# First attention of a five-stage kernel: the last 65 keys' output products packed into two matmuls, the denominators into one

## The chip, the cores and the metric

One core of a Trainium2 chip runs the whole kernel; the other cores are idle. The metric is device time in microseconds for one execution: the median of the runs. TensorE appears as PE in the profile (its weight loads as PEld), VectorE as DVE, ScalarE as ACT, GpSimd as POOL, SyncE, which issues most DMAs, as SP.

## The reference

The kernel computes a chain of six residual stages on x (8 batches x 64 rows x 512). Only the first, a grouped cross-attention over a context of 1601 keys per batch, is touched:

```
q = (layernorm(x) @ Wq + bq)  -> 8 groups of 4 heads, head size 128
k, v = split(ctx @ Wkv + bkv) -> 8 key/value heads
attn = softmax(q k^T / sqrt(128)) over the 1601 keys
x = x + (attn @ v) @ Wo + bo
```

The reference is in float32. A state-space stage, a ternary linear layer, an attention against the raw context, a self-attention and an octonion feed-forward layer follow; none of them is changed.

## The kernel before, in words

**Precision.** A float32 operand is split into a high part (rounded to the type `float32r`, which PE multiplies in one pass) and a low part (source minus high). `product` (L57) issues three matmuls: high*high, high*low, low*high (as L59, L60, L61 in the profile).

**Units.** The attention works in 64 units: 8 batches (`b`) times 8 key heads (`j`); a unit is one key head with its 4 query heads' 64 rows, 256 columns (`NQ`). The 1601 keys are 12 chunks of 128 and a last one of 65 (`rows`, L277). Chunks are grouped by two into `NG` = 7 groups and these into four `PIECES`; the last piece is the 65-key chunk alone.

**Work of a unit.** PE makes the keys from the context in four tiles (`key_tile`, 402, 402, 402 and 396 columns), for each pair of units the values (`value_tile`), the scores, and in `attend` the outputs: 13 chunks with three matmuls each, L59 to L61, then the denominators (`denominators`, L584 and L585: ones times the high and the low part of the partial sums). The softmax is done on ACT (copies, exponentials, high parts `pt_hi`), DVE (maxima, subtraction, sums, low parts of keys and values) and POOL (low parts `pt_lo` at L479, `sum_lo` at L492). The values of the 65 last keys were computed before and lie in DRAM; for each pair of units SP loads them with one DMA (L393) and POOL splits them (`split_on_pool`, L1017 and L1019).

**Order.** Each engine's order is written out by hand in a function `group(b, j, last)`, one call for each unit; engines are tied by semaphores. `attend(b, j - 1)` runs in `group(b, j)`: right after the scores when j is odd, after the four key tiles of the next unit when j is even. POOL's order in a group is: weights and queries of unit j + 2 (`key_weights`), for even j the values of the last keys (`rest_values`, which waits for the end of PE's attention), `low`, `sum_low`, for j = 6 the split of the next batch's context (`split_ctx`, L472 and L474, four tiles with two raw buffers: the load of tile 2 waits for the split of tile 0), for even j the value weights (L443, L445). PE's first product with a new context is key tile 0 in the group j = 7, after `attend(b, 6)`; each tile waits for its own split (`ctx_lo_set`). There are seven such changes of batch.

Of the kernel before, what the change touches and what calls it, by code (L numbers as in the profile page):

```python
# [70 lines left out]
class Context:  # L71


    def __init__(self, nc, scope, ctx_t):
# [7 lines left out]
        self.pad_set, self.hi_set, self.lo_set = (scope.sem(n) for n in ("pad_set", "hi_set", "lo_set"))  # L82
# [177 lines left out]
def cross_attention(nc, context, early, rest, output, s_ps, st, wk, wv, ident, q_dram, o_dram):  # L260
# [47 lines left out]
    with Scope(nc, "xa") as sc:  # L308
# [66 lines left out]
        def _(sp):  # L375
# [63 lines left out]
        def _(pool):  # L439
# [24 lines left out]
            def split_ctx(b, n):  # L464

                for t, (c, w) in enumerate(TILES):
# [4 lines left out]
                    raw, hi, lo = context.parts(t)  # L471
                    nc.gpsimd.tensor_scalar(hi, raw, 1.0, 1.0, ALU.mult, ALU.mult).then_inc(ctx_hi_set, 1)  # L472
                    pool.wait_ge(ctx_hi_set, n * NT + t + 1)
                    nc.gpsimd.tensor_tensor(lo, raw, hi.bitcast(F32), ALU.subtract).then_inc(ctx_lo_set, 1)  # L474
# [20 lines left out]
            def first():  # L495
                for i in range(2):
# [4 lines left out]
                nc.gpsimd.memset(ones_r[:, :].bitcast(F32), 1.0)  # L501
                nc.gpsimd.memset(st[:, :, NG - 1, :, :], 0.0).then_inc(ready, 1)
# [20 lines left out]
        def _(pe):  # L523
# [67 lines left out]
            def attend(b, j, between=None, alone=False):  # L591
# [4 lines left out]
                for p, (a, z) in enumerate(PIECES):  # L596
# [62 lines left out]
        def _(act):  # L659
# [2928 lines left out]
```

## Time and profile before

| | us |
|---|---|
| median of 3 runs | 2588.86 (2587.87 to 2589.98) |
| the profiled execution | 2592.26 |
| its span, first to last instruction | 2590.5 |
| PE busy | 2494.6 (96%) |
| DVE busy | 1723.8 (67%) |
| ACT busy | 1486.7 (57%) |
| POOL busy | 1350.5 (52%) |

The attention fills the span from about 130 to 1885 us. In 40 slices of the span PE's row reads 9 from slice 1 to 28 and its granted clock is at full speed there.

### The profile page before, as it was taken

Reading aid. Unit: us, or ns where it says so; the run is one execution under the profiler, and the core shown is the slowest. Engines: PE = TensorE matmul, PEld = TensorE weight load, DVE = VectorE, ACT = ScalarE, POOL = GpSimd, SP = SyncE. Lnnn points to the kernel's source line nnn. Section 1 sums busy time; section 2 is a strip of 40 time slices with the busy share of each in tenths; the row PEclk is TensorE's granted clock in tenths of the full one; section 3 lists DMA queues with packets and bytes.
Section 4 is the critical chain, followed back from the end, with each engine's and each line's share of the span. In section 5 each row is a group of like instructions: output and inputs, shape, how many; then the busy total and the mean of one; then the engine's idle time right before and its main releaser. Section 6 shows DMA issues by size and latency. Waiting matters only on the chain. (4 is left out here: it accounts for less than half of the span.)

```text
span 2590.5 us, 42412 instructions
## 1 busy us (share of the span) xinstructions
PE 2494.6 (96%) x17112; PEld 2289.4 (88%) x17112; DVE 1723.8 (67%) x1950; ACT 1486.7 (57%) x2591; POOL 1350.5 (52%) x1009
## 2 busy tenths in 40 slices
PE   8999999999999999999999999999999699889889
PEld 6899999999999999999999999999977477754557
DVE  4157766777667777677776777766756699843573
ACT  3356655666555666556665566655643677622672
POOL 3335585475566458447555645845510499400352
PEclk9999999999999999999999999999999699989889
DMA  6521011111111101102111120100251300188200
GB/s 222 191 69 39 26 60 52 43 52 52 35 38 49 59 26 60 52 29 66 52 35 29 49 69 26 58 28 27 94 196 54 131 1 1 53 302 307 96 1 16
DMA packets 106986, 184.41 MB, mean 71 GB/s; under 512 B 8852, under 2 KB 69588, under 8 KB 105004
## 3 DMA queue, kind: packets, MB, share of 16 engines
q1 hardware_dynamic: 98476, 173.38, 20.0%
q10 hardware_dynamic: 8320, 8.39, 1.0%
q8 instruction: 133, 2.18, 0.4%
q14 instruction: 57, 0.47, 0.1%
HBM read 161.72 MB, written 20.02 MB: 70 GB/s over the span
## 5 line engine op out<-in xcount | busy, mean ns | idle before, releaser
L479 POOL TENSOR_TENSOR xa_pt_lo<-xs_st,xa_pt_hi 128x1024 fp32r<-128x1024 f32 x255 | 508.4, 2031 | 486.9 <-ACT xa_pt_hi L696 486.9
L59 PE MATMUL ctx_kv_ps<-ctx_wv_hi,ctx_hi 128*128 128x256 f32 x1536 | 431.8, 281 | 0.0
L61 PE MATMUL ctx_kv_ps<-ctx_wv_hi,ctx_lo 128*128 128x256 f32 x1536 | 430.2, 280 | 0.0
L60 PE MATMUL ctx_kv_ps<-ctx_wv_lo,ctx_hi 128*128 128x256 f32 x1536 | 430.2, 280 | 0.0
L59 PE MATMUL ctx_kv_ps<-ctx_hi,ctx_wk_hi 128*128 128x402 f32 (+1 forms) x1024 | 358.5, 350 | 1.8 <-DVE xa_k_lo L796 1.8
L60 PE MATMUL ctx_kv_ps<-ctx_lo,ctx_wk_hi 128*128 128x402 f32 (+1 forms) x1024 | 354.3, 346 | 0.0
L61 PE MATMUL ctx_kv_ps<-ctx_hi,ctx_wk_lo 128*128 128x402 f32 (+1 forms) x1024 | 353.2, 345 | 0.0
L803 DVE TENSOR_TENSOR xa_v_lo<-ctx_kv_ps,xa_v_hi 128x512 fp32r<-128x512 f32 x192 | 132.8, 692 | 244.1 <-ACT xa_v_hi L670 243.4
L60 PEld LDWEIGHTS ctx_kv_ps<-ctx_wv_lo,ctx_hi 128*128 128x128 f32 x1536 | 289.7, 189 | 0.0
L59 PEld LDWEIGHTS ctx_kv_ps<-ctx_wv_hi,ctx_hi 128*128 128x128 f32 x1536 | 288.6, 188 | 0.0
L61 PEld LDWEIGHTS ctx_kv_ps<-ctx_wv_hi,ctx_lo 128*128 128x128 f32 x1536 | 288.4, 188 | 0.0
L837 DVE TENSOR_TENSOR xs_st<-xs_st,xa_m_ps 128x1024 f32<-128x1024 f32 (+1 forms) x256 | 254.0, 1014 | 46.0 <-PE xa_m_ps L580 42.3
L670 ACT ACTIVATE xa_v_hi<-ctx_kv_ps 128x512 fp32r<-128x512 f32 x192 | 115.0, 599 | 288.0 <-PE ctx_kv_ps L61 288.0
L678 ACT ACTIVATE xs_st<-xs_s_ps 128x512 f32<-128x512 f32 (+1 forms) x448 | 262.9, 604 | 29.3
L691 ACT ACTIVATE xs_st<-xs_st 128x1024 f32<-128x1024 f32 (+1 forms) x256 | 228.3, 904 | 65.6 <-DVE xs_st L837 56.9
L664 ACT ACTIVATE xa_k_hi<-ctx_kv_ps,ctx_bk_sb 128x402 fp32r<-128x402 f32 (+1 forms) x256 | 152.2, 595 | 150.9 <-PE ctx_kv_ps L61 143.1
L59 PE MATMUL xa_o_ps<-xa_pt_hi,xa_v_hi 128*128 128x256 f32 (+1 forms) x832 | 238.0, 286 | 0.5 <-DVE xa_pt_lo L861 0.5
L696 ACT ACTIVATE xa_pt_hi<-xs_st 128x1024 fp32r<-128x1024 f32 (+1 forms) x256 | 237.3, 965 | 0.1
L60 PE MATMUL xa_o_ps<-xa_pt_lo,xa_v_hi 128*128 128x256 f32 (+1 forms) x832 | 235.2, 283 | 0.0
L61 PE MATMUL xa_o_ps<-xa_pt_hi,xa_v_lo 128*128 128x256 f32 (+1 forms) x832 | 235.1, 283 | 0.0
L61 PE MATMUL xs_s_ps<-xa_q_hi,xa_k_lo 128*128 128x256 f32 (+1 forms) x832 | 234.6, 282 | 0.0
L59 PE MATMUL xs_s_ps<-xa_q_hi,xa_k_hi 128*128 128x256 f32 (+1 forms) x832 | 234.0, 281 | 0.0
(517 smaller groups left out, 6335.3 us busy)
## 6 DMA issues: line engine op xcount, KB each, us to landing
ctx_raw<-in_ctx_t SPq DMA_DIRECT2D x24, 804.0 KB, 6.8
ctx_wk_raw<-in_xa_wk SPq DMA_DIRECT2D x64, 256.0 KB, 2.8
ctx_wv_raw<-in_xa_wv SPq DMA_DIRECT2D x32, 512.0 KB, 4.4
n_back<-in_ctx SPq DMA_DIRECT2D x8, 1280.0 KB, 10.7
q_raw<-in_xa_wq SPq DMA_DIRECT2D x8, 1024.0 KB, 5.0
q_scratch<-q_q_sb ACTq DMA_DIRECT2D x8, 1024.0 KB, 4.4
ctx_q_raw<-q_scratch SPq DMA_DIRECT2D x64, 128.0 KB, 2.7
o_scratch<-xa_o_sb SPq DMA_DIRECT2D x64, 128.0 KB, 1.7
```

The source lines that it names most:

```text
L59: nc.tensor.matmul(out, left[0], right[0], start=first, stop=False)
L60: nc.tensor.matmul(out, left[0], right[1], start=False, stop=False)
L61: return nc.tensor.matmul(out, left[1], right[0], start=False, stop=last)
L479: nc.gpsimd.tensor_tensor(by_chunk(pt_lo, p), scored(j, p).rearrange("p g q c -> p g c q"), by_chunk(pt_hi, p).bitcast(F32), ALU.subtract) ...
L664: nc.scalar.activation(k_hi[:, c:c + w], kv_ps[:, n % 2, 0:w], ACT.Identity, bias=bk_sb[:, j % NKV:j % NKV + 1]).then_inc(kv_hi, 1)
L670: nc.scalar.activation(v_hi[:, 2 * g:2 * g + 2, :], kv_ps[:, n % 2, :].rearrange("p (c d) -> p c d", c=2), ACT.Copy).then_inc(kv_hi, 1)
L678: nc.scalar.activation(st[0:r, j % 2, g, :, 0:m].rearrange("p q c -> p c q"), s_ps[0:r, g % NSLOT, 0:m * NQ].rearrange("p (c q) -> p c q", ...
L691: nc.scalar.activation(t, t, ACT.Exp, scale=SCALE).then_inc(exp_set, 1)
L696: nc.scalar.activation(by_chunk(pt_hi, p), scored(j, p).rearrange("p g q c -> p g c q"), ACT.Copy).then_inc(hi_set, 1)
L803: nc.vector.tensor_tensor(v_lo[:, 2 * g:2 * g + 2, :], kv_ps[:, n % 2, :].rearrange("p (c d) -> p c d", c=2), v_hi[:, 2 * g:2 * g + 2, :]. ...
L837: nc.vector.tensor_tensor(t, t, m_ps[0:r, 1, :].unsqueeze(1).unsqueeze(3).broadcast_to([r, g, q, m]), ALU.add).then_inc(sub_set, 1)
```

## The change

The context gets 1602 columns: the last key is copied into the pad instead of zeros, so the last chunk has 66 rows. Its output products become two matmuls instead of three. The first multiplies high values (64 keys, stored twice) with the high and, in rows 64 to 127, the low probabilities. The second has rows 0 to 63 with low values and high probabilities, and the 65th key's three terms in rows 64, 65 and 96. ACT writes the high parts twice in one instruction; POOL subtracts for the low parts in two instructions (64 rows, one row), and builds the second value operand with two multiplications by a per-partition mask and an addition. SP loads the values of the last keys with five DMAs instead of one. For the denominators ACT copies the upper 64 rows of the sums down, DVE adds the two halves (`folded`), POOL writes their high part into rows 0 to 63 and their low part into rows 64 to 127, and PE makes one matmul. DVE's sum leaves the last group out of its reduction and adds the 65 rows in an instruction of its own. At the start POOL sets masks and zeros (8 small memsets) and one large memset of `st` goes.

```
-        for part in (self.hi, self.lo):
-            self.nc.gpsimd.memset(part[:, :, self.S:self.SE].bitcast(F32), 0.0).then_inc(self.pad_set, 1)
-        pool.wait_ge(self.pad_set, 2)
         for t in range(len(self.TILES)):
             pool.wait_ge(self.loaded[t], 16)
-            src, hi, lo = self.parts(t)
-            self.nc.gpsimd.tensor_scalar(hi, src, 1.0, 1.0, ALU.mult, ALU.mult).then_inc(self.hi_set, 1)
-            pool.wait_ge(self.hi_set, t + 1)
-            self.nc.gpsimd.tensor_tensor(lo, src, hi.bitcast(F32), ALU.subtract).then_inc(self.lo_set, 1)
+            self.split(pool, t, t + 1)
+
+    def split(self, pool, t, count):
+
+        nc = self.nc
+        src, hi, lo = self.parts(t)
+        last = t == len(self.TILES) - 1
+        if last:
+            pad = slice(self.S, self.SE)
+            end = src[:, :, self.S - self.TILES[t][0] - 1:self.S - self.TILES[t][0]]
+            nc.gpsimd.tensor_scalar(self.hi[:, :, pad], end, 1.0, 1.0, ALU.mult, ALU.mult)
+        nc.gpsimd.tensor_scalar(hi, src, 1.0, 1.0, ALU.mult, ALU.mult).then_inc(self.hi_set, 1)
+        pool.wait_ge(self.hi_set, count)
+        if last:
+            nc.gpsimd.tensor_tensor(self.lo[:, :, pad], end, self.hi[:, :, pad].bitcast(F32), ALU.subtract)
+        nc.gpsimd.tensor_tensor(lo, src, hi.bitcast(F32), ALU.subtract).then_inc(self.lo_set, 1)
...
+    LAST = NC - 1
+    REST, ROWS = S - LAST * P, SE - LAST * P
+    EVEN = REST - 1
+    ALONE = 3 * P // 4
...
+        v_rest, pt_rest = sc.sb("v_rest", [P, 2, 2 * D], F32R), sc.sb("pt_rest", [P, 2, NQ], F32R)
...
+                values = rest.dram[j % NKV // 2, at:at + REST]
                 if n > 0:
                     sp.wait_ge(rest_split, n)
-                sp.dma_start(rest_v[0:r, :], rest.dram[j % NKV // 2, at:at + r]).then_inc(rest_in, 16)
+                else:
+                    sp.wait_ge(rest_clear, 1)
+                sp.dma_start(rest_v[0:EVEN, 0, :], values[0:EVEN]).then_inc(rest_in, 16)
+                sp.dma_start(rest_v[EVEN:2 * EVEN, 0, :], values[0:EVEN]).then_inc(rest_in, 16)
+                sp.dma_start(rest_v[0:REST, 1, :], values).then_inc(rest_in, 16)
+                sp.dma_start(rest_v[REST:ROWS, 1, :], values[EVEN:REST]).then_inc(rest_in, 16)
+                sp.dma_start(rest_v[ALONE:ALONE + 1, 1, :], values[EVEN:REST]).then_inc(rest_in, 16)
...
+                    context.split(pool, t, n * NT + t + 1)
...
             def low(b, j, start=0):
-                for p in range(start, NP):
+                for p in range(start, NP - 1):
                     pool.wait_ge(hi_set, unit(b, j) * NP + p + 1)
                     nc.gpsimd.tensor_tensor(by_chunk(pt_lo, p), scored(j, p).rearrange("p g q c -> p g c q"),
                                             by_chunk(pt_hi, p).bitcast(F32), ALU.subtract).then_inc(lo_set, 1)
+                pool.wait_ge(hi_set, unit(b, j) * NP + NP)
+                pool.wait_ge(lo_set, unit(b, j) * NP + NP - 1 - start)
+                nc.gpsimd.tensor_tensor(pt_rest[EVEN:2 * EVEN, 0, :], rest_scores(j, 0, EVEN),
+                                        pt_rest[0:EVEN, 0, :].bitcast(F32), ALU.subtract).then_inc(rest_low, 1)
+                pool.wait_ge(rest_low, unit(b, j) + 1)
+                nc.gpsimd.tensor_tensor(pt_rest[ALONE:ALONE + 1, 1, :], rest_scores(j, EVEN, REST),
+                                        pt_rest[EVEN:REST, 1, :].bitcast(F32), ALU.subtract).then_inc(lo_set, 1)
+                pool.wait_ge(lo_set, unit(b, j) * NP + NP - start)
 
             def rest_values(b, j):
                 n = unit(b, j)
-                r = rows(NC - 1)
-                pool.wait_ge(rest_in, (n // 2 + 1) * 16)
+                m = n // 2 + 1
+                pool.wait_ge(rest_in, m * 80)
                 pool.wait_ge(o_full, n + 1)
-                split_on_pool(nc, pool, v_hi[0:r, NC - 1, :], v_lo[0:r, NC - 1, :], rest_v[0:r, :], rest_hi_set,
-                              n // 2 + 1).then_inc(rest_split, 1)
+                nc.gpsimd.tensor_scalar(v_rest[:, :, :], rest_v[:, :, :], 1.0, 1.0, ALU.mult, ALU.mult).then_inc(rest_high, 1)
+                pool.wait_ge(rest_high, m)
+                nc.gpsimd.tensor_scalar(rest_v[:, 1, :], rest_v[:, 1, :], of_raw[:, 0:1], None, ALU.mult).then_inc(rest_part, 1)
+                nc.gpsimd.tensor_scalar(rest_h[:, :], v_rest[:, 1, :].bitcast(F32), of_high[:, 0:1], None,
+                                        ALU.mult).then_inc(rest_part, 1)
+                pool.wait_ge(rest_part, 2 * m)
+                nc.gpsimd.tensor_tensor(v_rest[:, 1, :], rest_v[:, 1, :], rest_h[:, :], ALU.add).then_inc(rest_split, 1)
 
             def sum_low(b, j):
-                pool.wait_ge(sum_hi_set, unit(b, j) + 1)
-                nc.gpsimd.tensor_tensor(sum_lo[:, :], sums[:, 1, :], sum_hi[:, :].bitcast(F32),
+                n = unit(b, j)
+                pool.wait_ge(fold_set, n + 1)
+                if n > 0:
+                    pool.wait_ge(o_full, n + 1)
+                nc.gpsimd.tensor_scalar(sum_halves[0:HP, :], upper[:, :], 1.0, 1.0, ALU.mult,
+                                        ALU.mult).then_inc(sum_hi_set, 1)
+                pool.wait_ge(sum_hi_set, n + 1)
+                nc.gpsimd.tensor_tensor(sum_halves[HP:P, :], upper[:, :], sum_halves[0:HP, :].bitcast(F32),
                                         ALU.subtract).then_inc(sum_lo_set, 1)
+                pool.wait_ge(sum_lo_set, n + 1)
...
             def denominators(b, j, alone=False):
                 pe.wait_ge(sum_lo_set, unit(b, j) + 1)
-                nc.tensor.matmul(d_ps(j, alone), ones_r[:, :], sum_hi[:, :], start=True, stop=False)
-                return nc.tensor.matmul(d_ps(j, alone), ones_r[:, :], sum_lo[:, :], start=False, stop=True)
+                return nc.tensor.matmul(d_ps(j, alone), ones_r[:, :], sum_halves[:, :], start=True, stop=True)
...
-                    for c in range(2 * a, min(2 * z, NC)):
-                        r = rows(c)
-                        end = product(nc, o_ps[:, j % 2, 0:NQ], (v_hi[0:r, c, d], v_lo[0:r, c, d]),
-                                      (pt_hi[0:r, c], pt_lo[0:r, c]), c == 0, c == NC - 1)
+                    for c in range(2 * a, min(2 * z, LAST)):
+                        product(nc, o_ps[:, j % 2, 0:NQ], (v_hi[:, c, d], v_lo[:, c, d]), (pt_hi[:, c], pt_lo[:, c]),
+                                c == 0, False)
+                    if p == NP - 1:
+                        nc.tensor.matmul(o_ps[:, j % 2, 0:NQ], v_rest[:, 0, d], pt_rest[:, 0], start=False, stop=False)
+                        end = nc.tensor.matmul(o_ps[:, j % 2, 0:NQ], v_rest[0:ALONE + 1, 1, d], pt_rest[0:ALONE + 1, 1],
+                                               start=False, stop=True)
...
+                if p == NP - 1:
+                    nc.scalar.activation(pt_rest[0:ROWS, :, :],
+                                         rest_scores(j, 0, ROWS).unsqueeze(1).broadcast_to([ROWS, 2, NQ]),
+                                         ACT.Copy).then_inc(hi_set, 1)
+                    return
                 nc.scalar.activation(by_chunk(pt_hi, p), scored(j, p).rearrange("p g q c -> p g c q"),
                                      ACT.Copy).then_inc(hi_set, 1)
 
-            def sum_high(b, j):
-                n = unit(b, j)
-                act.wait_ge(sum_set, n + 1)
-                if n > 0:
-                    act.wait_ge(o_full, n + 1)
-                nc.scalar.activation(sum_hi[:, :], sums[:, 1, :], ACT.Copy).then_inc(sum_hi_set, 1)
+            def upper_sums(b, j):
+                act.wait_ge(sum_set, unit(b, j) + 1)
+                nc.scalar.activation(upper[:, :], sums[HP:P, 1, :], ACT.Copy).then_inc(upper_set, 1)
...
+            def with_rest(b, j):
+                dve.wait_ge(sum_main, unit(b, j) + 1)
+                nc.vector.tensor_tensor(sums[0:REST, 1, :], sums[0:REST, 1, :], rest_scores(j, 0, REST),
+                                        ALU.add).then_inc(sum_set, 1)
+
             def summed(b, j):
                 dve.wait_ge(exp_set, unit(b, j) * NP + NP)
                 dve.wait_ge(sum_lo_set, unit(b, j))
-                over_chunks(sums[:, 1, :], j, 0, NG, ALU.add).then_inc(sum_set, 1)
+                over_chunks(sums[:, 1, :], j, 0, NG - 1, ALU.add).then_inc(sum_main, 1)
+                with_rest(b, j)
...
+            def folded(b, j):
+                dve.wait_ge(upper_set, unit(b, j) + 1)
+                nc.vector.tensor_tensor(upper[:, :], sums[0:HP, 1, :], upper[:, :], ALU.add).then_inc(fold_set, 1)
...
                     key_tile(b, j + 1, 2)
+                    if not alone:
+                        folded(b, j - 1)
                     shifted(b, j, 0)
...
                         value_tile(b, j, g)
+                        if g == 2:
+                            folded(b, j)
```

## Rows read from the trace of the kernel before

**Rows 1.** Busy time by stretch, mid-attention: length, PE, PEld, DVE, ACT, POOL, clock, DMA, GB/s.
```profile
800.00:1000.00 200.00, 200.00 (x1518) 199.82 (x1517) 137.91 (x147) 118.52 (x187) 118.43 (x89) 1.00 0.14 45
```

**Rows 2.** Instructions in order, PE, end of an attention: start, us, then what.
```profile
748.77 0.28 PE L59 MATMUL xa_o_ps<-xa_pt_hi,xa_v_hi 128*128 128x256 f32 x1
...
753.08 0.28 PE L59 MATMUL xa_o_ps<-xa_pt_hi,xa_v_hi 65*128 65x256 f32 x1
...
753.44 0.28 PE L584 MATMUL xa_o_ps<-xa_sum_hi,xa_ones_r 128*128 128x256 f32 x1
...
753.67 0.29 PE L59 MATMUL ctx_kv_ps<-ctx_wv_hi,ctx_hi 128*128 128x256 f32 x1
```

**Rows 3.** Instructions in order, POOL: the denominators' low part in that attention.
```profile
749.41 0.76 POOL L492 TENSOR_TENSOR xa_sum_lo<-xa_sums,xa_sum_hi 128x256 fp32r<-128x256 f32 x1
```

**Rows 4.** Instructions in order, POOL, up to the first change of batch.
```profile
314.93 0.75 POOL L492 TENSOR_TENSOR xa_sum_lo<-xa_sums,xa_sum_hi 128x256 fp32r<-128x256 f32 x1
...
318.11 0.74 POOL L445 TENSOR_TENSOR xa_q_lo<-ctx_q_raw,xa_q_hi 128x256 fp32r<-128x256 f32 x1
319.52 0.40 POOL L1017 TENSOR_SCALAR xa_v_hi<-xa_rest_v 65x256 fp32r<-65x256 f32 x1 [0.68 <-PE xa_o_ps L585]
320.01 0.74 POOL L1019 TENSOR_TENSOR xa_v_lo<-xa_rest_v,xa_v_hi 65x256 fp32r<-65x256 f32 x1
321.05 7.98 POOL L479 TENSOR_TENSOR xa_pt_lo<-xs_st,xa_pt_hi 128x1024 fp32r<-128x1024 f32 x4 [0.30 <-ACT xa_pt_hi L696]
329.04 0.74 POOL L492 TENSOR_TENSOR xa_sum_lo<-xa_sums,xa_sum_hi 128x256 fp32r<-128x256 f32 x1
329.74 1.54 POOL L472 TENSOR_SCALAR ctx_hi<-ctx_raw 128x1608 fp32r<-128x1608 f32 x1
```

**Rows 5.** Instructions in order, POOL: the split of context tile 3, all seven changes.
```profile
346.83 2.99 POOL L474 TENSOR_TENSOR ctx_lo<-ctx_raw,ctx_hi 128x1580 fp32r<-128x1580 f32 x1
...
566.22 2.99 POOL L474 TENSOR_TENSOR ctx_lo<-ctx_raw,ctx_hi 128x1580 fp32r<-128x1580 f32 x1
...
781.47 3.00 POOL L474 TENSOR_TENSOR ctx_lo<-ctx_raw,ctx_hi 128x1580 fp32r<-128x1580 f32 x1
...
999.43 3.00 POOL L474 TENSOR_TENSOR ctx_lo<-ctx_raw,ctx_hi 128x1580 fp32r<-128x1580 f32 x1
...
1216.41 2.99 POOL L474 TENSOR_TENSOR ctx_lo<-ctx_raw,ctx_hi 128x1580 fp32r<-128x1580 f32 x1
...
1433.04 3.00 POOL L474 TENSOR_TENSOR ctx_lo<-ctx_raw,ctx_hi 128x1580 fp32r<-128x1580 f32 x1
...
1650.22 2.99 POOL L474 TENSOR_TENSOR ctx_lo<-ctx_raw,ctx_hi 128x1580 fp32r<-128x1580 f32 x1
```

**Rows 6.** Instructions in order, PE: first product of key tile 3 (changes 1, 2, 7).
```profile
352.67 0.34 PE L59 MATMUL ctx_kv_ps<-ctx_hi,ctx_wk_hi 128*128 128x396 f32 x1
...
569.90 0.34 PE L59 MATMUL ctx_kv_ps<-ctx_hi,ctx_wk_hi 128*128 128x396 f32 x1
...
1656.06 0.34 PE L59 MATMUL ctx_kv_ps<-ctx_hi,ctx_wk_hi 128*128 128x396 f32 x1
```

**Rows 7.** Groups of POOL by shape: busy us, mean ns, idle before.
```profile
L443 POOL TENSOR_SCALAR ctx_wk_hi<-ctx_wk_raw 128x512 fp32r<-128x512 f32 x62 | 38.8, 626 | 4.3 <-PE ctx_kv_ps L61 4.3
L1688 POOL TENSOR_SCALAR mamba_a_c_diag<-all_ident,mr_nrm 128x128 f32<-128x128 f32 x20 | 11.9, 612 | 57.1 <-DVE mr_nrm L1734 57.1
L2914 POOL TENSOR_TENSOR sa_hm_half<-sa_hm 128x4 f32<-128x4 f32 x1 | 0.4, 368 | 0.0
```

**Rows 8.** Instructions in order, PE: the end of its one pause at the attention's start.
```profile
136.56 0.42 PE L59 MATMUL ctx_kv_ps<-ctx_hi,ctx_wk_hi 128*128 128x402 f32 x1 [1.84 <-DVE xa_k_lo L796]
```

**Rows 9.** Busy time by stretch, after that pause, and in the last attention.
```profile
136.00:142.00 6.00, 5.44 (x21) 5.45 (x22) 1.59 (x3) 0.75 (x2) 2.50 (x5) 0.72 0.75 230
...
1880.00:1884.00 4.00, 3.72 (x24) 3.45 (x25) 2.88 (x4) 1.11 (x3) 2.73 (x3) 1.00 0.11 39
```

**Rows 10.** Instructions in order, PE, in the last attention.
```profile
1880.28 0.39 PE L584 MATMUL xa_m_ps<-xa_sum_hi,xa_ones_r 128*128 128x256 f32 x1 [1.41 <-POOL xa_sum_lo L492]
```

More of the change, by code:

```diff
@@ L81, in __init__ @@
         self.loaded = [scope.sem(f"loaded{t}") for t in range(len(self.TILES))]
-        self.pad_set, self.hi_set, self.lo_set = (scope.sem(n) for n in ("pad_set", "hi_set", "lo_set"))
+        self.hi_set, self.lo_set = (scope.sem(n) for n in ("hi_set", "lo_set"))
     def parts(self, t):
@@ L314, in cross_attention @@
         k_hi, k_lo = sc.sb("k_hi", [P, SE], F32R), sc.sb("k_lo", [P, SE], F32R)
-        v_hi, v_lo = sc.sb("v_hi", [P, NC, 2 * D], F32R), sc.sb("v_lo", [P, NC, 2 * D], F32R)
-        pt_hi, pt_lo = sc.sb("pt_hi", [P, NC, NQ], F32R), sc.sb("pt_lo", [P, NC, NQ], F32R)
+        v_hi, v_lo = sc.sb("v_hi", [P, LAST, 2 * D], F32R), sc.sb("v_lo", [P, LAST, 2 * D], F32R)
+        pt_hi, pt_lo = sc.sb("pt_hi", [P, LAST, NQ], F32R), sc.sb("pt_lo", [P, LAST, NQ], F32R)
+        v_rest, pt_rest = sc.sb("v_rest", [P, 2, 2 * D], F32R), sc.sb("pt_rest", [P, 2, NQ], F32R)
         mx, sums = sc.sb("mx", [P, 2, NQ]), sc.sb("sums", [P, 2, NQ])
-        sum_hi, sum_lo = sc.sb("sum_hi", [P, NQ], F32R), sc.sb("sum_lo", [P, NQ], F32R)
+        HP = P // 2
+        upper = sc.sb("upper", [HP, NQ])
+        sum_halves = sc.sb("sum_halves", [P, NQ], F32R)
         nmx = sc.sb("nmx", [P, NU])
@@ L338, in cross_attention @@
             sc.sem(n) for n in ("mx_step", "mx_set", "mt_full", "nmx_set", "diag_set", "bm_full"))
-        sub_set, exp_set, hi_set, sum_part, sum_set, lo_set, lo_dve = (
-            sc.sem(n) for n in ("sub_set", "exp_set", "hi_set", "sum_part", "sum_set", "lo_set", "lo_dve"))
-        sum_hi_set, sum_lo_set = sc.sem("sum_hi_set"), sc.sem("sum_lo_set")
+        sub_set, exp_set, hi_set, sum_part, sum_main, sum_set, lo_set, lo_dve = (
+            sc.sem(n) for n in ("sub_set", "exp_set", "hi_set", "sum_part", "sum_main", "sum_set", "lo_set", "lo_dve"))
+        upper_set, fold_set, sum_hi_set, sum_lo_set = (sc.sem(n) for n in ("upper_set", "fold_set", "sum_hi_set", "sum_lo_set"))
         o_full, sum_full, rden_set, on_set, o_free = (
@@ L344, in cross_attention @@
         o_out = output.o_out
-        rest_v = sc.sb("rest_v", [P, 2 * D])
-        rest_in, rest_hi_set, rest_split = (sc.sem(n) for n in ("rest_in", "rest_hi_set", "rest_split"))
+        rest_v, rest_h = sc.sb("rest_v", [P, 2, 2 * D]), sc.sb("rest_h", [P, 2 * D])
+        of_raw, of_high = sc.sb("of_raw", [P, 1]), sc.sb("of_high", [P, 1])
+        rest_clear, rest_in, rest_split, rest_low, rest_high, rest_part = (
+            sc.sem(n) for n in ("rest_clear", "rest_in", "rest_split", "rest_low", "rest_high", "rest_part"))
+        mask_set = sc.sem("mask_set")
         block = sc.block()
@@ L353, in scored, with rest_scores @@
                 return st[:, j % 2, a:z, :, :]
-            return st[0:rows(NC - 1), j % 2, a:z, :, 0:1]
+            return st[0:ROWS, j % 2, a:z, :, 0:1]
         def by_chunk(t, p):
             a, z = PIECES[p]
-            if z < NG:
-                return t[:, 2 * a:2 * z, :].rearrange("p (g c) q -> p g c q", c=2)
-            return t[0:rows(NC - 1), NC - 1:NC, :].unsqueeze(2)
+            return t[:, 2 * a:2 * z, :].rearrange("p (g c) q -> p g c q", c=2)
+        def rest_scores(j, a, z):
+            return st[a:z, j % 2, NG - 1, :, 0]
         def d_ps(j, alone=False):
@@ L470, in split_ctx @@
                     apart(pool, passed)
[L471 to L474, printed above, removed]
+                    context.split(pool, t, n * NT + t + 1)
             def low(b, j, start=0):
-                for p in range(start, NP):
+                for p in range(start, NP - 1):
                     pool.wait_ge(hi_set, unit(b, j) * NP + p + 1)
@@ L493, in sum_low @@
                                         ALU.subtract).then_inc(sum_lo_set, 1)
+                pool.wait_ge(sum_lo_set, n + 1)
             def first():
+                nc.gpsimd.memset(rest_v[EVEN:P, 1, :], 0.0).then_inc(rest_clear, 1)
+                pool.wait_ge(rest_clear, 1)
+                nc.gpsimd.memset(pt_rest[EVEN:P, 1, :].bitcast(F32), 0.0).then_inc(rest_clear, 1)
+                pool.wait_ge(rest_clear, 2)
+                for t, most in ((of_raw, 1.0), (of_high, -1.0)):
+                    nc.gpsimd.memset(t[:, :], most).then_inc(mask_set, 1)
@@ L496, in first @@
+                pool.wait_ge(mask_set, 2)
+                for at in (EVEN, ALONE):
+                    for t, one in ((of_raw, 0.0), (of_high, 1.0)):
+                        nc.gpsimd.memset(t[at:at + 1, :], one).then_inc(mask_set, 1)
+                pool.wait_ge(mask_set, 6)
                 for i in range(2):
@@ L500, in first @@
                     pool.wait_ge(early.q_out[i], (NKV // 2 + 1) * 16)
-                nc.gpsimd.memset(ones_r[:, :].bitcast(F32), 1.0)
-                nc.gpsimd.memset(st[:, :, NG - 1, :, :], 0.0).then_inc(ready, 1)
+                nc.gpsimd.memset(ones_r[:, :].bitcast(F32), 1.0).then_inc(ready, 1)
                 group(0, 0, False)
@@ L927, in group @@
                     summed_in_two(b, j, 1)
+                    folded(b, j)
                     normalise(b, j - 1)
```

18 lines of the change are left out of this document (9 added, 9 removed).

## Prediction, made before the changed kernel was run

> **What bounds the kernel now.** I read the stretches by busy time first. In the 200 us from 800 to 1000, PE is busy for all 200, with its weight loads at 199.8 and the clock at 1.00; DVE stands at 138, ACT at 119, POOL at 118, DMA at 14% [rows 1]. The attention is bound by the number of PE's matmuls and by nothing else, as long as nobody is late for PE. So there are two questions: what is one matmul worth, and how much slack has each engine whose work grows. The instructions in order answer the first: 36 matmuls of 256 columns start between 748.77 and 753.08, 0.120 us apart, although each is shown 0.28 us long; the two for the denominators take 0.115 each [rows 2]. The 65-row ones keep the same step, so rows cost nothing and only the count matters.
>
> For the second I follow POOL, which gets nearly all the new work, in order of time. In a usual pair of units it has room: it finishes the low part of the denominators at 750.17 for a matmul that PE starts at 753.44 [rows 2, 3]. But at a change of batch it works without a rest from 329.74 on, splitting four context tiles, and PE waits for each of them. Split 3 ends at 349.82 and PE starts on it at 352.67 [rows 5, 6]. The seven slacks (PE's starts are 217.23 us apart) are 2.85, 0.69, 2.66, 1.93, 2.19, 2.78 and 2.85 us, 15.95 in sum [rows 5, 6]. The second is small because its raw tile landed late. This is the place where POOL's extra work can reach PE.
>
> **PE's gain.** 64 units lose one output matmul (3 to 2) and one for the denominators (2 to 1): 64 x 0.120 + 64 x 0.115 = 15.1 us less [rows 2]. The two packed ones use up to 128 rows instead of 65, at no cost by the same rows.
>
> **POOL's extra work, up to the splits.** Own durations: a subtraction of 256 columns takes 0.74, an immediate multiplication 0.40, and an instruction that waits for POOL's own previous one starts 0.09 after its end (319.52 + 0.40 against 320.01), where independent ones follow 0.04 before it [rows 4].
> - Last piece and denominators, each unit: two subtractions of 0.74 + 0.70 become three subtractions, one multiplication and five gaps: 3 x 0.74 + 0.41 + 5 x 0.09 = 3.08. That is 3.08 - 1.40 = 1.68 later. The one-row subtraction I price like the others, since 65 rows and 128 rows both take 0.74 [rows 4]; its floor is 0.37, the four-column one [rows 7].
> - At a change this counts twice. The first time (unit 5) it eats the 0.67 us in which POOL idled before the values of the last keys (318.85 to 319.52), so these begin 1.01 later [rows 4].
> - Values of the last keys: 0.40 + 0.09 + 0.74 = 1.23 becomes one of 512 columns (0.63), a gap, two mask multiplications, a gap and an addition (0.74) [rows 4, 7]. The masks are multiplications by a per-partition scalar. The trace has twenty of that form on POOL, of 128 columns, at 0.61 us each, dearer than an immediate one of 256 (0.40) [rows 4, 7]. For 256 columns I take 0.80; the bounds are 0.40 (as the immediate) and 1.22 (twice the row). Sum 3.15, so 1.92 more, less the 0.30 us in which POOL waited for ACT: the low parts start 1.01 + 1.92 - 0.30 = 2.63 later.
> - Unit 6's last piece and denominators: 1.68 more, 4.31. Two small instructions for the pad before split 3 ends: 0.2 each (floor zero, ceiling 0.37 [rows 7]): 4.7 us late in all. The load of raw tile 2 waits for split 0, so it moves by as much and does not help.
>
> PE comes there earlier by four of the removed matmuls (0.47), and restarts about 0.1 late. So the pause in each change is 4.7 + 0.57 = 5.27 less the slack: 2.4, 4.6, 2.6, 3.3, 3.1, 2.5, 2.4, together 7 x 5.27 - 15.95 = 20.9 us.
>
> The Trainium skill speaks against my price for the masks: "GPSIMD Engine Reference", section "Engine selection", calls one-input operations on GpSimd roughly line-rate. Nothing there makes a scalar operand dearer, and the masks would then stand at about the 0.40 us of the immediate form; that is the second rival below. The row of 0.61 us for 128 columns speaks against the rule, so my sum goes by the row.
>
> **The clock.** Before the attention PE paused 1.84 us once, and over the 6 us from 136 to 142 the granted clock averaged 0.72: part of that time ran at 1.2 instead of 2.4 GHz, 6 x 0.28 = 1.7 us lost [rows 8, 9]. After the pause of 1.41 us in the last attention it stayed at 1.00 [rows 9, 10]. All seven new pauses are longer than 1.84. One case each way is no law: none would cost 0, all seven 11.9; I take four, 6.8 us.
>
> **The last attention.** Here PE already waits 1.41 us for POOL's `sum_lo` [rows 10]. The chain grows by the same 1.68 (ACT's copy takes the place of its old one), less a matmul or two on PE: 1.5 us.
>
> **What I cost at nothing.** DVE's reduction gets 512 of its input columns shorter and an addition of 256 columns longer, and one more such addition (`folded`) stands before a subtraction that waits for PE anyway; if that cover were gone, 0.4 to 0.7 us a unit would be DVE's, which idles 62 of 200 us [rows 1]. ACT's last high part doubles to 512 columns, with 81 of 200 us free. SP's four more DMAs for each pair lie behind its store; POOL needs them some 25 us later. The weights that are queued behind them come 2 us later, with over 10 us in hand. Queued behind POOL's new waits stand the next weights: those of unit 9 are split 4.7 later, while PE's need of them moves by its own pause. The start: eight small memsets, one large one less, before a `ready` that PE needs after two more key tiles.
>
> **Sum**, on the profiled execution (2592.26, its span 2590.5, 1.8 around it): -15.1 + 20.9 + 6.8 + 1.5 = +14.1. The median lies 3.4 under the profiled time; I put the difference on it: 2588.86 + 14.1 = 2603.0.
>
> **Rivals.**
> - *As forecast* (0.46): POOL is late at the seven changes; 2594 to 2612 on its own (masks half a microsecond apart in sum: 3.5 either way; none to seven falls of the clock).
> - *Masks cheap* (0.24): 0.40 each, so POOL is 0.8 less late. Pauses 7 x 4.47 - 15.95 = 15.3, two falls of the clock 3.4: -15.1 + 15.3 + 3.4 + 1.5 = +5.1, 2594. For it: POOL's immediate rows. Against: the row with a scalar operand.
> - *The gain stays* (0.20): the lateness never reaches PE. It decides whether POOL comes later than 0.7 to 2.9 us at split 3. If the one-row subtraction and the masks cost little and the idle stretches absorb the rest, only -15.1 + 1.5 = -13.6 is left: 2575. For it: POOL is busy for only 118 of 200 us [rows 1], and in usual pairs it does absorb. Against: the rows show no idle between 321.05 and the splits.
> - *Dearer* (0.10): masks at 1.22 and a fall of the clock after every pause: -15.1 + 26.5 + 11.9 + 1.5 = +24.8, 2614.
>
> That the matmuls do not go away is no rival: the count is fixed by the loop.
>
> **Numbers.** 0.2% is 5.2 us, about what a measurement of this kernel tells from no change. Slower by more: most of the forecast (0.42), all of "dearer" (0.10), nearly half of "masks cheap" (0.11): 0.63. Within: the rest of these two, 0.17. Faster: 0.20. The range goes down to 2582, to take in "masks cheap" and a lateness that is partly absorbed, and up to 2612.
>
> **What would show it.** PE's matmuls fall by 128. At the seven changes (first near 350) PE waits for POOL's `ctx_lo` at key tile 3, 2.4 to 4.6 us each; if it waits less than 1 us, my chain is wrong. POOL's mask multiplications take 0.8 us; at 0.4 the second rival holds. Between the changes PE has no wait; if it waits in every pair for `pt_rest` or `sum_halves`, the usual slack was misread. The granted clock shows dips just behind the pauses. At the end the wait for the denominators is near 2.9 us.

## The result and the profile after

Before: 2589.98 us (median of 5 runs, 2587.87 to 2591.82). After: 2603.43 us (5 runs, 2599.80 to 2607.97). The ratio is 1.0055, 95% interval 1.0040 to 1.0069: the change costs 13 to 14 us. The profiled execution took 2602.36 us, its span 2600.6. One execution of experiment 3 took 6435.98 us at a granted clock of 0.375 and is left out of its median and ratio.

The first part of the page, busy time and number of instructions of each engine:

```profile
PE 2480.7 (95%) x16984; PEld 2271.7 (87%) x16984; DVE 1844.5 (71%) x2078; ACT 1503.5 (58%) x2591; POOL 1499.0 (58%) x1222
```

PE lost 128 matmuls and 14 us of busy time, as it should. POOL gained 149 us, which was expected, and DVE 121 us, which was not.

What PE waits for between 100 and 1900 us: in sum, how often, the longest.

```profile
PE ctx_kv_ps L59 <- POOL ctx_lo L114: 19.4, 14, 2.4
PE xa_m_ps L639 <- POOL xa_sum_halves L536: 2.9, 1, 2.9
PE ctx_kv_ps L59 <- DVE xa_k_lo L855: 1.8, 1, 1.8
PE ctx_kv_ps L59 <- DVE xa_v_lo L862: 1.8, 2, 1.4
PE xa_o_ps L59 <- DVE xa_pt_lo L931: 0.8, 1, 0.8
```

The first line is new, and is the largest part of the loss. The instructions in order on PE show where it sits. Each change of batch has a small wait at key tile 2 and one of 2.4 us at tile 3; two of seven changes, a wait of DVE's in the first unit, and the last attention:

```profile
169.43 0.39 PE L59 MATMUL ctx_kv_ps<-ctx_wv_hi,ctx_hi 128*128 128x256 f32 x1 [1.38 <-DVE xa_v_lo L862]
...
351.06 0.45 PE L59 MATMUL ctx_kv_ps<-ctx_hi,ctx_wk_hi 128*128 128x402 f32 x1 [0.27 <-POOL ctx_lo L114]
...
355.92 0.70 PE L59 MATMUL ctx_kv_ps<-ctx_hi,ctx_wk_hi 128*128 128x396 f32 x1 [2.41 <-POOL ctx_lo L114]
356.42 0.53 PE L60 MATMUL ctx_kv_ps<-ctx_lo,ctx_wk_hi 128*128 128x396 f32 x1
...
1668.28 0.45 PE L59 MATMUL ctx_kv_ps<-ctx_hi,ctx_wk_hi 128*128 128x396 f32 x1 [2.41 <-POOL ctx_lo L114]
...
1892.93 0.39 PE L639 MATMUL xa_m_ps<-xa_sum_halves,xa_ones_r 128*128 128x256 f32 x1 [2.94 <-POOL xa_sum_halves L536]
```

In [rows 6] the first and the seventh tile 3 start at 352.67 and 1656.06; here at 355.92 and 1668.28. The batch takes 218.73 us for 217.23, though it has 1.9 us (8 x 0.236) less of matmuls: each change costs 3.4 us. POOL at the first change, against [rows 4] and the first of [rows 5]:

```profile
318.19 0.63 POOL L471 TENSOR_SCALAR ctx_wk_hi<-ctx_wk_raw 128x512 fp32r<-128x512 f32 x1 [0.22 <-POOL xa_sum_halves L536]
...
321.35 0.62 POOL L520 TENSOR_SCALAR xa_v_rest<-xa_rest_v 128x512 fp32r<-128x512 f32 x1
322.07 0.92 POOL L522 TENSOR_SCALAR xa_rest_v<-xa_rest_v,xa_of_raw 128x256 f32<-128x256 f32 x1
322.98 0.93 POOL L523 TENSOR_SCALAR xa_rest_h<-xa_v_rest,xa_of_high 128x256 f32<-128x256 f32 x1
323.99 0.75 POOL L526 TENSOR_TENSOR xa_v_rest<-xa_rest_v,xa_rest_h 128x256 fp32r<-128x256 f32 x1
324.69 7.44 POOL L504 TENSOR_TENSOR xa_pt_lo<-xs_st,xa_pt_hi 128x1024 fp32r<-128x1024 f32 x3
332.28 0.75 POOL L508 TENSOR_TENSOR xa_pt_rest<-xs_st,xa_pt_rest 64x256 fp32r<-64x256 f32 x1
333.10 0.74 POOL L511 TENSOR_TENSOR xa_pt_rest<-xs_st,xa_pt_rest 1x256 fp32r<-1x256 f32 x1
...
335.37 1.54 POOL L110 TENSOR_SCALAR ctx_hi<-ctx_raw 128x1608 fp32r<-128x1608 f32 x1 [0.23 <-POOL xa_sum_halves L536]
...
352.88 2.98 POOL L114 TENSOR_TENSOR ctx_lo<-ctx_raw,ctx_hi 128x1580 fp32r<-128x1580 f32 x1
```

The splits begin at 335.37 for 329.74 and end at 355.86 for 349.82, where PE stands ready.

DVE's busy time is in two new groups (busy us, mean ns), both additions of two SBUF tiles that take 0.40 and 0.42 us where nothing holds them:

```profile
L927 DVE TENSOR_TENSOR xa_upper<-xa_sums,xa_upper 64x256 f32<-64x256 f32 x64 | 108.6, 1696 | 0.5 <-ACT xa_upper L763 0.5
...
L901 DVE TENSOR_TENSOR xa_sums<-xa_sums,xs_st 65x256 f32<-65x256 f32 x64 | 61.6, 963 | 2.2
```

The second in ns, shortest, median and longest:

```profile
L901 DVE TENSOR_TENSOR xa_sums<-xa_sums,xs_st x64: 422/1204/2451, 166.4 to 1889.1; 65x256 f32<-65x256 f32 x64
```

### The profile page after: what moved, and what is told of

It is laid out like the page before. It is cut to its first block and busy times, and to the rows that moved or that the text cites. A ratio compares the mean times of both kernels' runs of the same rounds, so it can differ in the third digit from the quotient of the medians.

```text
span 2600.6 us, 42754 instructions
## 1 busy us (share of the span) xinstructions
PE 2480.7 (95%) x16984; PEld 2271.7 (87%) x16984; DVE 1844.5 (71%) x2078; ACT 1503.5 (58%) x2591; POOL 1499.0 (58%) x1222
## 5 line engine op out<-in xcount | busy, mean ns | idle before, releaser
L504 POOL TENSOR_TENSOR xa_pt_lo<-xs_st,xa_pt_hi 128x1024 fp32r<-128x1024 f32 x191 | 468.2, 2480 | 454.4 <-ACT xa_pt_hi L758 454.4
L59 PE MATMUL ctx_kv_ps<-ctx_hi,ctx_wk_hi 128*128 128x402 f32 (+1 forms) x1024 | 360.1, 352 | 21.2 <-POOL ctx_lo L114 19.4
L855 DVE SCALAR_TENSOR_TENSOR xa_k_lo<-ctx_kv_ps,ctx_bk_sb,xa_k_hi 128x402 fp32r<-128x402 f32 (+1 forms) x256 | 161.9, 633 | 123.7 <-ACT xa_k_hi L721 123.7
L60 PE MATMUL xs_s_ps<-xa_q_lo,xa_k_hi 128*128 128x256 f32 (+1 forms) x832 | 233.1, 280 | 0.0
L867 DVE TENSOR_REDUCE xa_m_ps<-xs_st 128x256 f32<-128x1536 f32 (+1 forms) x97 | 188.2, 1940 | 53.0 <-ACT xs_st L735 48.9
L59 PE MATMUL xa_o_ps<-xa_pt_hi,xa_v_hi 128*128 128x256 f32 x768 | 216.9, 282 | 0.8 <-DVE xa_pt_lo L931 0.8
```

Of the source, the lines that this page charges most:

```text
L59: nc.tensor.matmul(out, left[0], right[0], start=first, stop=False)
L60: nc.tensor.matmul(out, left[0], right[1], start=False, stop=False)
L855: nc.vector.scalar_tensor_tensor(out=k_lo[:, c:c + w], in0=kv_ps[:, n % 2, 0:w], scalar=bk_sb[:, j % NKV:j % NKV + 1], in1=k_hi[:, c:c + w ...
L867: return nc.vector.tensor_reduce(out, st[:, j % 2, a:z, :, :].rearrange("p g q c -> p q g c"), AX_XY, op)
```

## The experiments

Ratios are to the kernel before on the same chip; it took 2590.07 us beside experiments 1 to 4, 2589.47 beside 5 to 8 and 2591.45 beside 9 to 11. "Pauses" is the line PE <- POOL `ctx_lo` of the waits.

**1 and 2. Lateness alone, in two places.**

```
# kernel before, group(b, j, last) on POOL, behind sum_low(b, j)
+ if j == NKV - 2 and not last:      # the second kernel: NKV - 4
+     for i in range(7):
+         nc.gpsimd.tensor_scalar(idle_t, idle_t, 1.0, 1.0, ALU.mult, ALU.mult).then_inc(idle_set, 1)
+         pool.wait_ge(idle_set, 7 * b + i + 1)
```

> The kernel before, with seven small GpSimd operations of 0.62 us (128x512, on a tile of its own, each waiting for the last; some 4.8 us) put ahead of the context split, in the group before each of the seven changes of the batch. Nothing else is touched, the 128 matmuls among them. Theory (the time of the change lies in TensorE waiting for the third key tile at the seven changes): each of these waits as in the kernel after, 2.4 us of idle time shown and 0.3 to 0.7 more at the tile before, so +18 to +23 us over before (about 2610), and more by 1.7 us for each fall of the clock. Rival (the cost is spread over the 64 units, by the stretched VectorE additions): these are absent here, so under +5 us.

> The same seven GpSimd operations, but two groups earlier in the batch (ahead of the value weights, where no context split follows). Theory: they fall into GpSimd's idle time and cost nothing, within 1 us of before. Rival (GpSimd's added work costs wherever it stands, as its share of TensorE's waits or of a shared port): +2 us or more, by the same 34 us of added busy time.

Measured: 2615.10 us, ratio 1.0097 (1.0080 to 1.0114), ahead of the splits; 2590.73, ratio 1.0000 (0.9991 to 1.0010), two groups earlier. The same 34 us of POOL cost 25 us or nothing. It is the place that counts. The pauses of the first kernel:

```profile
PE ctx_kv_ps L59 <- POOL ctx_lo L475: 15.2, 7, 2.7
```

Most of the rest is the clock. Two of the seven stretches behind a pause (PE's granted clock is the third number from the end):

```profile
353.20:359.20 6.00, 5.84 (x30) 5.85 (x31) 1.28 (x2) 1.89 (x4) 5.75 (x7) 0.72 0.22 62
574.40:580.40 6.00, 5.88 (x30) 5.88 (x31) 1.32 (x2) 1.82 (x4) 5.75 (x7) 0.72 0.24 74
```

A mean of 0.72 of 2.4 GHz means that part of the time ran at 1.2: 6 x 0.28 = 1.7 us lost. This happened at six of seven changes, 10 us in all. Taken apart, neither part is as expected: the pauses are one of 2.1 to 2.7 us at each change, with none at the tile before, and so below the 18 to 23 us; with six falls on top that range would have been 28 to 33 us, and 25 were measured. The kernel after has longer pauses and fewer falls. Its first and second change:

```profile
355.80:359.20 3.40, 3.28 (x10) 3.28 (x11) 0.00 (x0) 0.00 (x0) 3.32 (x3) 0.50 0.02 5
576.00:579.40 3.40, 3.40 (x22) 3.40 (x23) 0.30 (x1) 0.81 (x2) 3.32 (x3) 1.00 0.00 0
```

At 0.50 of 2.4 GHz matmuls of 396 columns are shown 0.53 us long for 0.34 (the row of 356.42 above). In this execution that happened once in seven.

**3 and 4. Each half of the change alone.** One kernel packs the last 65 keys and leaves `sum_high`, `sum_low` and both denominator matmuls as before; the other folds the denominators and leaves the three output matmuls.

> The packed last 65 keys alone; the denominators stay two products from sums halved by ScalarE and GpSimd. Theory: the product saves 64 x 0.120 = 7.7 us; GpSimd's context split starts some 3.2 us later at each change (value preparation 3.3 against 1.2 us, two small subtractions for one, the pads), which by the slacks read before makes 10.5 us of pauses: +3 us, about 2593. Rival (additions on VectorE are the cost): the second addition of each unit and the wait behind it are absent, so the waits at the third key tile would be as before and the time 2582.

> The folded denominators alone; the last 65 keys are multiplied as before in three products. Theory: saves 64 x 0.115 = 7.4 us, and GpSimd's split starts 0.5 to 1.7 us later at each change, mostly within its slack: 0.5 to 2.5 us of pauses, so -5 to -7 us, about 2584. Rival (spread cost of the VectorE additions, which stretch beside GpSimd's subtractions): the saving is lost, within 1 us of before or slower.

Measured: packing 2594.12 us, ratio 1.0019 (1.0009 to 1.0029), pauses 8.7; denominators 2580.55, ratio 0.9965 (0.9952 to 0.9977), no pause at all. The two differences, +5 and -9, don't add up to +13: each half has the slack of POOL to itself. The denominators stay within it, the packing overruns it by 8.7 us of pauses and both together by 19.4. The denominators alone gained about 2 us more than the removed matmuls were priced at. In the traces, from one unit's denominators matmul to the next and away from the changes, a unit is 0.15 us shorter with the denominators alone, 0.13 to 0.14 with the packing alone and 0.26 in the kernel after, where 0.115, 0.120 and 0.235 were priced. Why a matmul taken out gives more than the step between two of them stays open.

**5. The kernel after again.**

> The kernel after once more, for what differs between its own executions. Theory: the pauses at the seven changes are the same in each execution (2.4 us of idle time at the third key tile), and its spread of 2599.8 to 2608.0 us is the number of changes at which the granted clock falls, some 1.65 us each: where this profiled run has n of them, its time is near 2599 + 1.65 n, with the mean clock lower by 0.0006 for each. Rival: the pauses themselves vary between executions, with the transfers.

Measured: 2602.47 us (2600.74 to 2605.11), ratio 1.0047 (1.0033 to 1.0061). In its profiled execution (2605.11) the clock fell at three changes, and once more behind the wait for the denominators, where the matmul is shown 0.58 us long for 0.39. Pauses are 18.6 us. The end of the attention is 3.2 us later than in the first profile, with three falls more, 5.1 us by their price; the pauses shown are 0.8 us shorter, and about 1 us is not accounted for. So the pauses nearly stay and the falls vary, as expected. The formula is rough: with the three falls at changes it gives 2604.0, 1.2 short, having left out the last fall, and for the first profile, with one, 2600.7 for 2602.36.

**6 and 7. Take the preparation off the path, or shorten it.** Both make the halves of the second product with one mask of -1 (rows wanted low) and 0 (rows wanted high), rounding the product as it is written, three operations for four:

```
- tensor_scalar(v_rest[:, :, :], rest_v[:, :, :], 1.0, 1.0, ...)
- tensor_scalar(rest_v[:, 1, :], rest_v[:, 1, :], of_raw, ...)
- tensor_scalar(rest_h, v_rest[:, 1, :], of_high, ...)
+ tensor_scalar(v_rest[:, 0, :], rest_v[:, 0, :], 1.0, 1.0, ...)
+ tensor_scalar(rest_h, rest_v[:, 1, :], minus, ...)      # rest_h now float32r
  tensor_tensor(v_rest[:, 1, :], rest_v[:, 1, :], rest_h, ALU.add)
```

The first also does it one group earlier, in place in one of two buffers that the DMAs fill directly:

```
- if j % 2 == 0:
-     rest_values(b, j)
+ if unit(b, j) == 0:
+     rest_values(b, j)
+ if j % 2 and has_keys(j, last):
+     rest_values(b, j + 1)                 # values = v_rest[:, n // 2 % 2]
```

> The kernel after, with the values of the last 65 keys prepared one group earlier, in GpSimd's idle time of the odd group, into one of two buffers, and in three operations for four (the halves of the second product with one mask of -1 and 0, 0.40 + 0.92 + 0.74 us). Theory (lateness of GpSimd at the changes is the cost): 3.4 us fewer stand ahead of the context split, so it starts 1.3 us later than in the kernel before, within the slack of six of seven changes: at most 1.2 us of pauses; with the 15.1 saved, 1.9 us lost in the first unit and 1.5 at the end, -10 us, about 2579. Rival (the other added work, on VectorE and in the waits among GpSimd's small operations, costs by itself): at 2590 or more.

> The kernel after, with the values of the last 65 keys prepared where they were, in three operations for four (one mask of -1 and 0, applied to the raw values while they are rounded). Theory: 1.2 us fewer ahead of each context split, all of it on the path: each of the seven pauses is shorter by 1.2 us, -8 us against the kernel after, about 2595. Rival (the split is held by the arrival or the buffer of the context, not by GpSimd's own work): no change, 2603.

Measured: ahead 2578.83 us, ratio 0.9956 (0.9942 to 0.9970), no pauses. In place 2610.39, ratio 1.0078 (1.0063 to 1.0093): 8 us slower than the kernel after beside it (2602.47), against both theories. Its waits of PE:

```profile
PE ctx_kv_ps L59 <- DVE xa_v_lo L858: 19.1, 31, 1.4
PE ctx_kv_ps L59 <- POOL ctx_lo L114: 5.2, 7, 0.9
```

The pauses shrank, by 2 us each. But in 31 pairs of units PE now waits 0.6 us for a value tile, and such a pair is 0.81 to 0.89 us longer than in the kernel after, so the idle time shown is not the whole price: some 26 us in sum, against 18 won at the seven changes (1.7 of them a fall of the clock). DVE and POOL, in order, in one such pair:

```profile
438.30 0.42 DVE L918 TENSOR_TENSOR xa_sums<-xa_sums,xa_m_ps 128x256 f32<-128x256 f32 x1
438.76 2.63 DVE L897 TENSOR_TENSOR xa_sums<-xa_sums,xs_st 65x256 f32<-65x256 f32 x1
441.31 0.68 DVE L858 TENSOR_TENSOR xa_v_lo<-ctx_kv_ps,xa_v_hi 128x512 fp32r<-128x512 f32 x1
...
433.83 7.28 POOL L504 TENSOR_TENSOR xa_pt_lo<-xs_st,xa_pt_hi 128x1024 fp32r<-128x1024 f32 x3
441.26 0.73 POOL L508 TENSOR_TENSOR xa_pt_rest<-xs_st,xa_pt_rest 64x256 fp32r<-64x256 f32 x1
```

The addition at 438.76 ends at 441.39, just behind the end of POOL's third subtraction (433.83 + 7.28 = 441.11). The same pair in the kernel after:

```profile
440.68 1.44 DVE L901 TENSOR_TENSOR xa_sums<-xa_sums,xs_st 65x256 f32<-65x256 f32 x1
442.65 2.06 DVE L927 TENSOR_TENSOR xa_upper<-xa_sums,xa_upper 64x256 f32<-64x256 f32 x1
...
436.96 7.46 POOL L504 TENSOR_TENSOR xa_pt_lo<-xs_st,xa_pt_hi 128x1024 fp32r<-128x1024 f32 x3
```

Its three subtractions end near 439.4, 441.9 and 444.4; the two additions end at 442.12 and 444.71. So DVE's addition of two SBUF tiles stands still until POOL's running subtraction is done. All 64 instructions of L901 in the kernel after say the same: the 31 that meet no POOL instruction take 0.42 us, and the 33 that start beside a subtraction take 1.03 to 2.45 and end 0.28 behind its end. The length is a matter of when the two meet: 1.44 us in one kernel, 2.63 in the other, where POOL stands 1.2 us earlier against DVE (3.1 and 1.9 us earlier by the clock), by just the work that was saved. The addition just ahead, with one operand in PSUM, takes 0.42 beside the same subtraction.

The Trainium skill has this rule, "SBUF — State Buffer", section "Who interferes with whom": VectorE and GpSimd share one pair of SBUF ports, a VectorE instruction with two SBUF inputs contends for it with a GpSimd one that reads SBUF, and the later one blocks for the whole instruction of the other. The traces here agree: 0.42 us alone, up to 2.63 behind a subtraction of about 2.45.

**8. Such an addition by itself.** The kernel before with one idle DVE operation in each unit:

```
+ if n // 2 % 2 == 0: nc.vector.tensor_tensor(extra[:, 1, :], extra[:, 0, :], extra[:, 1, :], ALU.add)
+ else: nc.vector.tensor_scalar(extra[:, 1, :], extra[:, 0, :], 1.0, 1.0, ALU.mult, ALU.mult)
```

> The kernel before, with one VectorE operation more in each unit of 65x256 on a tile of its own, right behind the sums: in every second pair of units an addition of two tiles, in the others a multiplication of one tile by 1. Theory (VectorE's operations with two inputs from SBUF are stretched while GpSimd works): the addition takes 1 us or more on the mean, the multiplication under 0.5. Rival (anything of VectorE is stretched there): both take about the same. For the time of the kernel: some 32 to 60 us more of VectorE's busy time, less than 3 us in the span by the theory that VectorE isn't on the path but in the first unit and at the end.

Measured: 2590.69 us, ratio 1.0004 (0.9994 to 1.0013). Both operations and their mean ns; then one of each in the order of time:

```profile
L847 DVE TENSOR_TENSOR xa_extra<-xa_extra 65x256 f32<-65x256 f32 x32 | 22.2, 694 | 0.0
L849 DVE TENSOR_SCALAR xa_extra<-xa_extra 65x256 f32<-65x256 f32 x32 | 17.1, 535 | 0.0
```

```profile
166.29 1.98 DVE L847 TENSOR_TENSOR xa_extra<-xa_extra 65x256 f32<-65x256 f32 x1
198.55 0.41 DVE L847 TENSOR_TENSOR xa_extra<-xa_extra 65x256 f32<-65x256 f32 x1
221.27 0.74 DVE L849 TENSOR_SCALAR xa_extra<-xa_extra 65x256 f32<-65x256 f32 x1
```

Less than expected on the mean (0.69 for 1 us or more), and the multiplication of one tile is held too. That fits neither theory as written. The mean only says how often the operation meets POOL: 16 additions that meet nothing take 0.41 us, 16 beside a subtraction of POOL's 0.88 to 1.98; 15 multiplications that meet nothing take 0.28, 17 beside one 0.48 to 0.80, and end 0.15 behind it. So the single-input form is not free of it. The one of the first unit stood still as in the kernel after (1.98 us, until 168.27, POOL's second subtraction ending near 168.1), and there PE waited 1.4 us for `v_lo`, as it does in the kernel after. In this trace PE is 1.5 us later behind the first unit and 1.0 at the attention's end; in the medians 1.2 us (2590.69 for 2589.47) can't be told from nothing.

**9 to 11. One operand in PSUM.** In even groups the last keys' sums go into the PSUM tile of partial sums, ahead of the addition that already reads it:

```
- nc.vector.tensor_tensor(sums[:, 1, :], sums[:, 0, :], m_ps[:, 1, :], ALU.add).then_inc(sum_main, 1)
- with_rest(b, j)
+ nc.vector.tensor_tensor(m_ps[0:REST, 1, :], m_ps[0:REST, 1, :], rest_scores(j, 0, REST), ALU.add).then_inc(sum_main, 1)
+ dve.wait_ge(sum_main, n + 1)
+ nc.vector.tensor_tensor(sums[:, 1, :], sums[:, 0, :], m_ps[:, 1, :], ALU.add).then_inc(sum_set, 1)
```

> The kernel with one mask (2610 us, slower than the kernel after by 7 us though its seven pauses fell from 2.4 to 0.7 us) with one more edit: in the even groups the last 65 keys' sums are added into the PSUM tile of partial sums, and not into the SBUF tile, so that this VectorE addition has one operand in SBUF and not two. Theory (an addition of two SBUF tiles on VectorE stands still until the running GpSimd subtraction ends, 2.63 us for 0.42, and makes TensorE wait 0.6 us for the low half of the value tile behind it in 31 groups): the addition takes 0.42 to 0.45 us, the 19.1 us of these waits go, about 2591. Rival (VectorE is late there for the number of its operations or for ScalarE's copies): the waits stay, 2605 to 2610.

> The kernel with the values prepared one group ahead and one mask (2578.8 us), with the same edit of the VectorE addition. Theory: of the stretched additions only that of the first unit reached TensorE (1.4 us, and 0.4 in the pace around it), so -1.4 to -1.9 us, about 2577. Rival: the fold of the sums behind it is stretched in its place and the first unit waits as before, 2578.8.

> The kernel after with that edit of the VectorE addition alone. Theory: in the kernel after the stretched addition (1.0 us on the mean) makes TensorE wait in the first unit only, so about 1.5 us less, 2601, and the seven pauses as they were. Rival (part of the pauses comes through VectorE): pauses shorter, 2597 or less.

Measured: with one mask 2589.11 us, ratio 0.9992 (0.9983 to 1.0002) for 1.0078, 22 us less. The waits for `v_lo` are gone (31 before). The moved addition, in that kernel:

```profile
L916 DVE TENSOR_TENSOR xa_m_ps<-xa_m_ps,xs_st 65x256 f32<-65x256 f32 x33 | 14.2, 429 | 1.1
```

0.43 us each, for up to 2.63: the standstill came from the second SBUF operand. The edit also moves the addition, but not out of POOL's way: of the 97 two-operand DVE instructions in this trace that read the PSUM tile and the score tile, 96 start beside a POOL subtraction, and none takes more than 0.43. The fold of the sums behind it (`folded`), still with two SBUF operands, takes 1.42 us on the mean. The pauses at the changes are 10.6 us, twice those of experiment 7, probably because there PE came to the changes late through its new waits, which hid part of POOL's lateness; that was not tested.

With the values ahead 2575.36 us, ratio 0.9939 (0.9926 to 0.9953), 3.5 us less than without the edit (4.4 by the ratios), where 1.4 to 1.9 were expected. In the two profiled executions the first unit gives 2.0 us, as expected; the next stage starts 3.2 earlier, and between the two lies the clock behind the last wait (0.57 on the mean from 1865 to 1873 us without the edit, 0.79 with it). All that PE still waits for in the attention:

```profile
PE xa_m_ps L640 <- POOL xa_sum_halves L536: 2.9, 1, 2.9
PE ctx_kv_ps L59 <- DVE xa_k_lo L857: 1.8, 1, 1.8
PE xa_o_ps L59 <- DVE xa_pt_lo L935: 0.8, 1, 0.8
PE ctx_kv_ps L59 <- PEq L30: 0.3, 1, 0.3
```

This is the best version, 16 us faster than before.

In the kernel after, the edit gives 2598.00 us, ratio 1.0032 (1.0021 to 1.0042), about 5 us less where 1.5 were expected. Two waits for `v_lo` go (1.8 us) and pauses fall from 19.4 to 18.1; in its profile the clock fell at no change and not in the stretch from 130 to 170 us, where the profile of after has one fall each (before has the latter too); it fell once behind the last wait instead (0.72 from 1886 to 1892 us), where after's did not. So of 4.8 us by which the next stage starts earlier 1.7 are the clock.

## Why the prediction was right

It named the mechanism, and the time within 0.5 us (2603.0 for 2603.4), and the second is in part luck. The sum was made on the profiled execution, where it says +14.1 and +10.1 was measured (2602.36 for 2592.26). There the clock took 5.1 us less than in the sum and the later stages gave 2.3, while the pauses, DVE and smaller items took some 3.5 more. The medians agree better only because the profiled execution of before lies 2.3 above its median and that of after 1.1 below. On the profiled executions, up to the next stage (PE's first matmul there at 1898.07 for 1885.66, +12.4 us):

| step | forecast | measured |
|---|---|---|
| PE's gain | -15.1 | -15.1 to -15.4 (experiment 10, without pauses: tile 3 at 348.94 and 564.25, a batch of 215.31 for 217.23, 1.92 less, times 8) |
| pauses at seven changes | +20.9 | +22 (3.4 each, less 0.3 for the share of the fall) |
| clock | +6.8 (four falls) | +1.7 (one fall); four in the second profile, three at changes and one behind the last wait |
| the first unit, DVE | 0 | +1.8 |
| the last attention | +1.5 | +1.5 (2.94 for 1.41), and 0.4 for `v_lo` |

With 0.3 us at the start that makes 12.6 with the smaller gain, 12.3 with the larger. Behind the attention the profiled execution of after gained 2.3 us on that of before, in stages that the change does not touch; the medians differ by 13.4.

- **Lateness of POOL, right, with its terms a little small.** Forecast 4.7 us; measured 6.0 at split 3, of which 0.7 is PE's own delay by then (POOL's first subtraction of unit 5 starts at 307.68 for 306.98): 5.3. The masks took 0.92 us and not 0.80, and behind `sum_halves` POOL idles 0.22 us more. "Masks cheap" (0.40) fell with the row of 0.92. Here the Trainium skill's "GPSIMD Engine Reference", section "Engine selection", would have misled: a one-input operation with a scalar for each partition took 924 ns for 256 columns, the immediate form 403. Experiments 1 and 2 show that lateness in this place is enough for the loss, experiment 6 that without it the gain stays.
- **Even pauses, wrong in the pattern.** By the slacks they should have been 2.4 to 4.6 us. They are 2.37 to 2.41 at tile 3 in all seven, with 0.2 to 0.7 at tile 2. Where PE waits at tile 2 already, the pause at tile 3 is only the difference between POOL's time for one tile and PE's, which is the same each time. The sum came out alike.
- **The clock, too many falls for the profiled execution.** The price of a fall (1.7 us) was right. The number isn't fixed: one and four in two executions of after, six in experiment 1 with shorter pauses, none at the changes in experiment 11 with pauses of 2.4 us.
- **"What I cost at nothing", the failed step: DVE.** I held 0.4 to 0.7 us a unit against its idle time. The two additions took 0.96 and 1.70 us on the mean, since each stands still behind POOL. In the kernel after this reaches PE in the first unit and once at the end only. Experiment 7 shows how near it was: POOL 1.2 us earlier against the same addition cost 19 us of waits, some 26 with what goes with them.
- **The rival "dearer"** has a small slip in its sum: masks at 1.22 us make pauses of 26.8 us, not 26.5. Nothing hangs on it.
- **The rival "the gain stays"** is the case of experiment 4 and 6: where the work ahead of the splits stays within POOL's slack, all of it is kept.

## What to carry to other kernels

Added work on an engine with idle time is priced at the one place where that engine is the last to arrive: the same 4.8 us, seven times, cost 25 us in all there and nothing two groups earlier. Halves of a change that use the same slack don't add up, so they are timed together. An addition of two SBUF tiles on VectorE beside a busy GpSimd is priced at GpSimd's running instruction, not at its own length; in these kernels an operand in PSUM took it out.

## What the hardware did that I had not expected

- VectorE's 0.42 us addition of two SBUF tiles took up to 2.63 us and ended 0.28 us behind GpSimd's running subtraction. With one operand in PSUM it took 0.43. Its multiplication of one SBUF tile was held as well, 0.28 to 0.80 us.
- A GpSimd multiplication by a per-partition scalar takes 0.92 us for 256 columns, by an immediate 0.40.
- A one-row GpSimd subtraction (748 ns) costs as much as one of 64 rows (746 ns), both of 256 columns.
- The granted clock fell to 0.50 behind a 2.4 us pause in one of seven changes, in three and in none of seven in two other profiles with such pauses, and behind pauses of 2.1 us in six of seven. What decides it stays open.
